# The next-to-last batch's output products: 8 plain single-precision matmuls in place of 24 split ones, with the weight sums made by GpSimd

## Chip, cores and metric

One core of one Trainium2 chip runs the whole kernel in one launch. The metric is the device time in microseconds; every time given for a kernel is a median over runs.

## The reference, cut to what matters

Sixteen sequences (here: batches) of 256 positions and 256 features go through two layers. In each, a normalised input goes through a mixing part `s` and a gate `g`, and `x + s * g` is the result. Layer 0 has a linear recurrence and an MLP. Layer 1, where the change lies, has causal attention over latents with 16 heads, and a gate of a dense product with LoRA experts:

```
kv = (c_kv @ Wkv_b).reshape(B, S, N_HEADS, QK_NOPE + V_DIM)
k_nope, v = (kv[..., :QK_NOPE], kv[..., QK_NOPE:])
...
attn = jax.nn.softmax(scores, axis=-1)
out = jnp.einsum('bhqk,bkhd->bqhd', attn, v).reshape(B, S, N_HEADS * V_DIM)
return out @ Wo
```

The kernel folds `Wkv_b`'s value part into `Wo` once (the folded weight lies in SBUF as 8 rows of 128x256), so that per batch it multiplies attention weights with the 64 latents of each position, and the result (1024 x 256 positions) with the folded weight. That last step is the output product.

## The kernel before

Every engine has one straight program; they meet through named semaphores alone. [...] A product of two single-precision matrices is done in one of two ways. In the split way each operand is a high part in float32r (names `_hi`, `h`) and a low part, the rest (names `_lo`, `l`), and `three` issues three float32r matmuls: low by high, high by low, high by high. In the plain way one float32 matmul does it (scores, transposes, attention by latents); the profile records a plain float32 matmul as two records.

Layer 1 runs in steps `n`, ten per batch (`UNITS`), 160 for the 16 batches, and a tail up to step 173. A step holds one unit of scores (a head pair's block of query rows) and whatever the tables put beside it. Batches overlap: while batch b's units of scores go, the queries of b+1 are made, the keys of b+1, the normalised input of b+2, and the latents and outputs of b-1. The unit kinds are W (2 tiles of 224 and 256 columns), M (3 tiles: 128, 160, 192) and T (transposed). For the batches 14 and 15 the table `LAST` gives the steps by hand: V (attention by latents), L (eviction of the latents), O (output product), R (gating) and C (residual).

Per unit n, in order: TensorE's `l1_s(n)` writes the scores into PSUM; VectorE's `most(n)` adds the mask, takes row minima and writes `SM`; ScalarE's `exps(n)` takes exponentials and their sums; VectorE's `inverse(n)` (two steps later); GpSimd's `normalise(n)` (same step), 2 or 3 instructions; VectorE's `turn_weights(n)` (four steps after the unit), which transposes into `PT`; then, when the units of a batch are all there, TensorE's `l1_pv`. `l1_s(n)` waits until `most(n-2)` is done.

Output, per batch and half of the positions (`qt`): ScalarE's `latents` evicts two banks each for two pairs into `oh` (high part), VectorE's `latents_low` subtracts that from PSUM into `ol` (low part), and `l1_out` makes the product, 8 rows of weight by 3 matmuls of 256 columns. `gated_out`, `residual` and a DMA follow. The products of batch 14 are numbers 28 and 29 (steps 159 and 161), those of batch 15 numbers 30 and 31. On TensorE the tail reads: scores 157, 158, 159; product 28; attention of batch 15, first part; product 29; attention of batch 15, last part; products 30 and 31.

Rotated queries go another way: VectorE's `turn_queries(b, g)` writes `QA`, GpSimd's `queries_sum` adds in place, and SyncE's `place` copies both sums of a half of the heads into `QT` with 8 DMAs, all on one semaphore (`d0` for the first half of batch 15). Here is the wait by which VectorE reuses `QA`:

```
w.wait_ge(*moved(turned[r - 2] // 2))
```

For sum g of batch 15, with g = 2 in step 147, it is the landing of all 8 DMAs with the sums g = 0 and 1 (GpSimd's steps 143 and 144).

Of the kernel before, what the change touches and what calls it, by code (L numbers as in the profile page):

```python
# [8 lines left out]
F32 = mybir.dt.float32  # L9
F32R = mybir.dt.float32r  # L10
I32 = mybir.dt.int32
ALU = mybir.AluOpType
ACT = mybir.ActivationFunctionType
AX = mybir.AxisListType

NB = 16
T = 256
D = 256
# [37 lines left out]
Q0_AT = {}  # L56
LAST_LORA, LAST_SUM, LAST_SPREAD = 152, 153, 149
FIRST_LORA, FIRST_SUM = 5, 6
KV_AT, GATE_AT, SCALE_AT, NORM_AT, YN_AT = 1, 2, 6, 0, 4
TURN_AT, TM_AT, TK_AT, LORA_AT, MISC_AT = 6, 6, 8, 8, (8, 9)  # L60
GATE_REST, FIRST_REST = 9, 22
# [23 lines left out]
    "wrl", "wnl", "wml", "lbl", "mtl", "wol", "bn1", "yn", "ytl", "kv", "kvw", "gt", "gsub", "gf", "z1", "w1",  # L85
    "st", "mx", "r", "qa", "pt", "otl", "ob",

    "gated", "clean", "par", "cs", "nu", "rr", "rt", "fill", "rl", "lr", "kr", "kvr", "n", "qq", "nw", "rs", "oc", "kwk", "kwv",
)


# [113 lines left out]
def build(nc, x, consts, rows, vecs, w1t, w2t, b1c, bt, ct, nuth, wqn, wkbt, wqr, wkva, wvbt, wo,  # L205
          baset, lorab, loraa, routert, out):
    ctx = ExitStack()
    with ctx:
# [112 lines left out]
        w1b = [spare[3], sb("w1b1", [128, 4, 128], F32, l1)]  # L321
        l1.close()

        PS = ctx.enter_context(nc.psum_tensor("bank", [128, 8, 512], F32))
        bank = [PS[:, i, :] for i in range(8)]
        tbank, fbank, obank, ubank, wbank = bank[0], (bank[1], bank[2]), (bank[4], bank[3], bank[6]), bank[5], bank[7]
# [20 lines left out]
        def freed_by(kind, i):  # L347
            if kind == "q":
                return [("qa", g_nth[i // 2]) if i % 2 else ("qn", n_nth[i // 2])]
            if kind == "v":  # L350
                last = max(EVAC.index((qt, i % 4 // 2)) for qt in range(2))
                return [("oth", 4 * (i // 4) + last + 1), ("otl", 4 * (i // 4) + last + 1)]
            if kind == "pad":
                return freed_by(*jorder[i - RING])
            return {"o": [("ob", i + 1)], "ty": [("yth", i + 1), ("ytl", i + 1)], "mi": [("mi", i + 1)],
                    "tk": [("kt", i + 1)], "tm": [("mt", i + 1), ("mtl", i + 1)], "lo": [("z1", i + 1)]}[kind]
# [28 lines left out]
        def evacuated(b, qt):  # L385

            return 4 * b + max(EVAC.index((qt, pair)) for pair in range(2)) + 1

        def normed_rows(b):

# [2 lines left out]
        def by_head(t, pair):  # L393
            return t[:, 4 * pair:4 * pair + 4, :].rearrange("p (i u) t -> p i u t", i=2)
# [158 lines left out]
        def _(e):  # L553
# [232 lines left out]
            def l1_pv(b, blocks, units):  # L786

                first, end = blocks
                C = C4[b % 2]
                w.wait_ge("pt", UNITS * b + units)  # L790
                w.wait_ge(f"c{b % 2}", 256 * (b // 2 + 1))
                for i in range(4):
                    free_shared("v", 4 * b + i)
                if blocks == LAST_BLOCKS:

                    w.wait_ge("otl", 4 * b + 2)
                for kb in range(end):
                    q = max(first, kb)
                    at = slice(64 * (kb % 2), 64 * (kb % 2) + 64)
                    for i in range(4):  # L800
                        rows_ = slice(32 * i, 32 * i + 32)
                        sums = jof("v", 4 * b + i).rearrange("p (u t) -> p u t", u=2)
                        for half in range(2):
                            j = e.matmul(sums[64 * half:64 * half + 64, :, 32 * q:32 * end],  # L804
                                         C[rows_, kb // 2, at], PT[rows_, 2 * half:2 * half + 2, kb, q:end, :],
                                         start=(kb == 0), stop=(kb == end - 1), skip_group_check=True)
                j.then_inc(SEM["pv"], 1)

            def l1_out(k):
                bk, qt = jof("o", k), k % 2  # L810
                w.wait_ge("oth", evacuated(k // 2, qt))
                w.wait_ge("otl", evacuated(k // 2, qt))
                w.wait_ge("woh", 4)
                w.wait_ge("wol", 4)
                free_shared("o", k)
                for c in range(8):
                    i = three(bk[:, 0:256], oh[qt][:, c, :], ol[qt][:, c, :], woe_hi[:, c, :], woe_lo[:, c, :],
                              c == 0, c == 7)
                i.then_inc(SEM["o"], 1)
# [113 lines left out]
        def _(e):  # L933
# [142 lines left out]
            def latents(b, qt):  # L1076
                w.wait_ge("pv", b + 1 + (b == NB - 1 and qt))
                if b == 0:
                    after_l0(w)
                for pair in range(2):  # L1080
                    i = EVAC.index((qt, pair))
                    w.wait_ge("o", 2 * (b - 1) + qt + 1)
                    if i > 1:
                        w.wait_ge("otl", 4 * b + i - 1)
                    e.activation(by_head(oh[qt], pair), latent_pair(b, qt, pair), ACT.Copy).then_inc(SEM["oth"], 1)

            def normed(b):
                w.wait_ge("rs", b + 1 if b > 1 else 1)
# [143 lines left out]
        def _(e):  # L1232
# [579 lines left out]
            for n in range(STEPS):  # L1812
                b, m = n // UNITS, n % UNITS
                for qt in range(2):
                    if (d := due("L", n, qt)) is not None:
                        latents_low(d, qt)
                c, i = divmod(n - 1, UNITS)
                if 0 <= c < NB - 2 and i == TURN_AT:
# [44 lines left out]
        def _(e):  # L1863
# [250 lines left out]
            def residual(k):  # L2114
                w.wait_ge("ob", k + 1)
                e.tensor_tensor(fo[k % 2][:, :], fo[k % 2][:, :], X[:, k, :], ALU.add).then_inc(SEM["oc"], 1)

            chain = iter(())
            for g in range(L0_STEPS):
                if g == 67:  # L2120
# [30 lines left out]
            for n in range(STEPS):  # L2151
# [17 lines left out]
                        residual(2 * d + qt)  # L2169
                if 0 <= n - 2 < TOTAL:  # L2170
                    normalise(n - 2)


def shape_constants():
# [86 lines left out]
```

## Time and profile before

| what | value |
|---|---|
| median of 3 runs | 789.76 us (789.55 to 789.94) |
| the profiled execution's own time | 789.47 us |
| its span (first to last instruction) | 787.7 us |
| busy share: PE, DVE, ACT, POOL | 99%, 86%, 66%, 61% |
| granted TensorE clock, mean | 1.000 (the 2.4 GHz level) |

PE is TensorE's matmuls, PEld its weight loads (beside the matmuls), DVE VectorE, ACT ScalarE, POOL GpSimd, SPq SyncE's queue of DMA issues. Times in rows are microseconds from the span's start unless they are in ns. A matmul record's own duration overlaps with its successor's; the pace is the distance between starts.

### The profile page before, as it was taken

The page shows a single profiled execution, that of the slowest core. Times are in us where ns is not written, and L with a number is a line of the kernel's source. Part 1 is how long each engine was busy: PE and PEld are TensorE (multiplying, and loading weights), DVE is VectorE, ACT ScalarE, POOL GpSimd, SP SyncE. Part 2 cuts the span into 40 slices and gives each one's busy share as a digit, 9 for nine tenths or more (in the row PEclk, how much of TensorE's full clock was granted, in tenths as well). Part 3 has the DMA queues.
Part 4 walks back from the last instruction along what each step waited for, and adds up shares of the span by engine and source line. Part 5 has one row for each costly group of instructions (what it writes and reads, how often), then busy time and mean ns, then how long its engine had stood idle before and what let it go on. Part 6 is the DMA issues. An engine that isn't in the chain of part 4 may idle for free.

```text
span 787.7 us, 23150 instructions
## 1 busy us (share of the span) xinstructions
PE 777.5 (99%) x7976; PEld 710.9 (90%) x7976; DVE 676.5 (86%) x2616; ACT 518.8 (66%) x1610; POOL 480.2 (61%) x1278
## 2 busy tenths in 40 slices
PE   9999999999999999999999999999999999999988
PEld 7889889888899989898998989999898998989867
DVE  6999897888687999888888988989889888989885
ACT  5554454545546687777768777687777768777682
POOL 6880202202236696776867668686776867767673
PEclk9999999999999999999999999999999999999999
DMA  8600220000002223222222322223222222322220
GB/s 305 252 2 1 60 78 34 1 1 1 1 15 50 47 42 58 54 54 36 49 49 45 60 45 52 39 46 58 53 55 35 48 43 49 58 48 53 34 52 28
DMA packets 101335, 41.16 MB, mean 52 GB/s; under 512 B 91745, under 2 KB 98401, under 8 KB 100577
## 3 DMA queue, kind: packets, MB, share of 16 engines
q1 hardware_dynamic: 99984, 39.15, 22.4%
q8 instruction: 63, 1.03, 0.5%
q10 hardware_dynamic: 1232, 0.52, 0.3%
q14 instruction: 56, 0.45, 0.2%
HBM read 14.47 MB, written 4.19 MB: 24 GB/s over the span
## 4 chain that ended last, share of the span: by engine, by line
PE 87%; DVE 5%; SPq 2%; POOL 2%; issue 1%; ACT 1%; DMA 1%; POOLq 0%; DVEq 0%; ACTq 0%
PE bank L558 60%; PE bank L782 11%; PE bank L804 8%; PE bank L775 2%; PE bank L638 2%; SPq L448 1%; SPq L519 1%; PE bank L575 1%; DVE SM L1612 1%; POOL SM L2054 1%; PE bank L690 1%; DVE PT L1635 1%; DVE QA L1583 1%; PE bank L650 1%; DVE ol L1657 1%
## 5 line engine op out<-in xcount | busy, mean ns | idle before, releaser
L1072 ACT ACTIVATE SM<-SM,stb 128x224 f32<-128x224 f32 (+7 forms) x512 | 206.0, 404 | 47.6 <-DVE stb L1612 47.0
L2054 POOL TENSOR_SCALAR SM<-SM,stb 128x224 f32<-128x224 f32 (+7 forms) x512 | 196.3, 406 | 53.8 <-DVE stb L1619 52.4
L558 PE MATMUL bank<-yh,wq_lo 128*128 128x256 f32 x512 | 150.3, 294 | 0.0
L558 PE MATMUL bank<-yh,wq_hi 128*128 128x256 f32 x512 | 144.3, 282 | 0.0
L558 PE MATMUL bank<-yl,wq_hi 128*128 128x256 f32 x512 | 144.2, 282 | 0.0
L782 PE MATMUL bank<-KT,QT 128*128 128x192 f32 (+4 forms) x640 | 118.6, 327 | 2.1 <-DVE stb L1612 2.1
L1635 DVE STREAM_TRANSPOSE PT<-SM 128x128 f32<-128x128 f32 (+2 forms) x232 | 99.3, 459 | 17.4 <-PE bank L804 17.4
L1612 DVE CUSTOM_DVE_ANT_0 SM<-bank,CONST 128x224 f32<-128x224 f32 (+3 forms) x320 | 97.1, 347 | 14.2 <-PE bank L782 10.3
L782 PEld LDWEIGHTS bank<-KT,QT 128*128 128x128 f32 x640 | 98.4, 190 | 6.2 <-DVE stb L1612 3.7
L558 PEld LDWEIGHTS bank<-yh,wq_lo 128*128 128x128 f32 x512 | 96.8, 189 | 1.4
L558 PEld LDWEIGHTS bank<-yl,wq_hi 128*128 128x128 f32 x512 | 96.8, 189 | 0.0
L558 PEld LDWEIGHTS bank<-yh,wq_hi 128*128 128x128 f32 x512 | 96.8, 189 | 0.0
L1072 ACT ACTIVATION_READ_ACCUMULATOR SM<-SM,stb 128x1 f32 x512 | 96.3, 188 | 0.0
L957 ACT ACTIVATE hs<-bank,B 128x512 f32<-128x512 f32 x64 | 43.9, 687 | 78.3 <-PE bank L558 77.3
L1044 ACT ACTIVATE QT<-bank 64x512 f32<-64x512 f32 x128 | 75.4, 589 | 7.2 <-issue 5.4
L1583 DVE TENSOR_TENSOR QA<-bank,TR 128x512 f32<-128x512 f32 x124 | 79.3, 681 | 0.3 <-DMA QT<-QA 0.3
L2047 POOL TENSOR_TENSOR QA<-QA 128x256 f32<-128x256 f32 x62 | 46.4, 749 | 53.9 <-DVE QA L1583 53.9
L558 PE MATMUL bank<-woe_hi,ol 128*128 128x256 f32 x256 | 75.4, 294 | 0.7 <-issue 0.7
L558 PE MATMUL bank<-w2h,hl 128*128 128x256 f32 x256 | 74.2, 290 | 0.3 <-DVE w2l L1356 0.2
L558 PE MATMUL bank<-w2h,hh 128*128 128x256 f32 x256 | 72.4, 283 | 0.0
L558 PE MATMUL bank<-w2l,hh 128*128 128x256 f32 x256 | 72.3, 283 | 0.0
L558 PE MATMUL bank<-woe_hi,oh 128*128 128x256 f32 x256 | 72.1, 282 | 0.0
(227 smaller groups left out, 2056.4 us busy)
## 6 DMA issues: line engine op xcount, KB each, us to landing
QT<-QA SPq DMA_DIRECT2D x244, 64.0 KB, 2.1
PT<-KV SPq DMA_DIRECT2D x256, 16.0 KB, 1.8
out<-fo SPq DMA_DIRECT2D x32, 128.0 KB, 2.0
X<-in_x SPq DMA_DIRECT2D x7, 512.0 KB, 11.0
stage<-in_wqn SPq DMA_DIRECT2D x2, 1024.0 KB, 5.2
stage<-in_wo SPq DMA_DIRECT2D x2, 1024.0 KB, 5.0
stage<-in_w1t SPq DMA_DIRECT2D x4, 256.0 KB, 5.3
stage<-in_w2t SPq DMA_DIRECT2D x2, 512.0 KB, 7.0
```

The costliest lines, as they stand in the source:

```text
L558: i = e.matmul(dst, a, b, start=(first and j == 0), stop=(last and j == 2), skip_group_check=skip)
L638: i = e.matmul(ubank[:, 256 * j:256 * j + 256], Z[b][:, 128 * j:128 * j + 128], RR[:, :], start=True, stop=True)
L782: j = e.matmul(sbank[n % 2][:, at], Q[:, q, :, :].rearrange("p h c -> p (h c)"), KT[b % 3][:, p, 0:32 * q + 32], start=True, stop=True)
L804: j = e.matmul(sums[64 * half:64 * half + 64, :, 32 * q:32 * end], C[rows_, kb // 2, at], PT[rows_, 2 * half:2 * half + 2, kb, q:end, :], ...
L957: e.activation(hs[g % 2][:, :], fbank[g % 2][:, :], ACT.Gelu, bias=B1[:, g % 8:g % 8 + 1]).then_inc(SEM["gelu"], 1)
L1044: i = e.activation(QT[r, (2 * b + g // 2) % 3, p, :, g % 2:4:2, :].rearrange("p n j c -> p j n c"), src[r, :, :, :], ACT.Copy)
L1072: i = e.activation(M[:, at], M[:, at], ACT.Exp, bias=S[:, 0, j:j + 1], scale=-1.0, accum_out=S[:, 1, j:j + 1])
L1583: i = e.tensor_tensor(A[:, part, :, :, g % 2, :], src, TR[:, part, :].rearrange("p (n c) -> p n c", n=8).unsqueeze(1).broadcast_to([128, 2 ...
L1612: i = e.tensor_tensor_reduce(M[:, at], bk[:, at], mask[:, 224 - 32 * q:256], 1.0, 3e38, ALU.add, ALU.min, S[:, 0, j:j + 1])
L1635: return e.transpose(PT[:, slot, 0:k, q:q + some, :].rearrange("p k q c -> p q k c"), src)
L2047: e.tensor_tensor(A[:, 0, 0, :, :], A[:, 0, 0, :, :], A[:, 1, 1, :, :], ALU.subtract)
L2054: i = e.tensor_scalar(P[:, at], P[:, at], S[:, 2, j:j + 1], 1.0, ALU.mult, ALU.mult)
```

## The change

For batch 14 alone, ScalarE evicts the latents in full single precision into `of` (which lies where `ol` did), VectorE's four subtractions go, and products 28 and 29 are 8 plain float32 matmuls each, of `of` with `whole`. `whole` is the folded weight in full, `woe_hi + woe_lo`, made by GpSimd in eight additions of 128x256, one at the end of each of its steps 141 to 148, in SBUF in which `yh1`, `yl1`, `yn0` and `yn1` have been used up by then. The counts on semaphore `otl` shift for batch 15 accordingly.

```diff
@@ -56,6 +56,7 @@
 Q0_AT = {}
 LAST_LORA, LAST_SUM, LAST_SPREAD = 152, 153, 149
 FIRST_LORA, FIRST_SUM = 5, 6
+WHOLE_AT = 141
 KV_AT, GATE_AT, SCALE_AT, NORM_AT, YN_AT = 1, 2, 6, 0, 4
 TURN_AT, TM_AT, TK_AT, LORA_AT, MISC_AT = 6, 6, 8, 8, (8, 9)
 GATE_REST, FIRST_REST = 9, 22
@@ -321,6 +322,17 @@
         w1b = [spare[3], sb("w1b1", [128, 4, 128], F32, l1)]
         l1.close()
 
+
+
+        l2 = ExitStack()
+        sb("gap3", [128, 512], F32, l2)
+        whole = [sb("whole0", [128, 2, D], F32, l2)]
+        sb("gap4", [128, 512], F32, l2)
+        whole += [sb(f"whole{i}", [128, 2, D], F32, l2) for i in range(1, 4)]
+        sb("gap5", [128, 28384], F32, l2)
+        of = [sb(f"of{i}", [128, 8, 128], F32, l2) for i in range(2)]
+        l2.close()
+
         PS = ctx.enter_context(nc.psum_tensor("bank", [128, 8, 512], F32))
         bank = [PS[:, i, :] for i in range(8)]
         tbank, fbank, obank, ubank, wbank = bank[0], (bank[1], bank[2]), (bank[4], bank[3], bank[6]), bank[5], bank[7]
@@ -349,7 +361,9 @@
                 return [("qa", g_nth[i // 2]) if i % 2 else ("qn", n_nth[i // 2])]
             if kind == "v":
                 last = max(EVAC.index((qt, i % 4 // 2)) for qt in range(2))
-                return [("oth", 4 * (i // 4) + last + 1), ("otl", 4 * (i // 4) + last + 1)]
+                if i // 4 == NB - 2:
+                    return [("oth", 4 * (i // 4) + last + 1)]
+                return [("oth", 4 * (i // 4) + last + 1), ("otl", lows(i // 4, last + 1))]
             if kind == "pad":
                 return freed_by(*jorder[i - RING])
             return {"o": [("ob", i + 1)], "ty": [("yth", i + 1), ("ytl", i + 1)], "mi": [("mi", i + 1)],
@@ -385,6 +399,11 @@
         def evacuated(b, qt):
 
             return 4 * b + max(EVAC.index((qt, pair)) for pair in range(2)) + 1
+
+        def lows(b, k):
+
+
+            return 4 * (b - (b == NB - 1)) + k
 
         def normed_rows(b):
 
@@ -793,7 +812,7 @@
                     free_shared("v", 4 * b + i)
                 if blocks == LAST_BLOCKS:
 
-                    w.wait_ge("otl", 4 * b + 2)
+                    w.wait_ge("otl", lows(b, 2))
                 for kb in range(end):
                     q = max(first, kb)
                     at = slice(64 * (kb % 2), 64 * (kb % 2) + 64)
@@ -809,7 +828,15 @@
             def l1_out(k):
                 bk, qt = jof("o", k), k % 2
                 w.wait_ge("oth", evacuated(k // 2, qt))
-                w.wait_ge("otl", evacuated(k // 2, qt))
+                if k // 2 == NB - 2:
+                    w.wait_ge("whole", 8)
+                    free_shared("o", k)
+                    for c in range(8):
+                        i = e.matmul(bk[:, 0:256], of[qt][:, c, :], whole[c // 2][:, c % 2, :], start=(c == 0),
+                                     stop=(c == 7))
+                    i.then_inc(SEM["o"], 1)
+                    return
+                w.wait_ge("otl", lows(k // 2, evacuated(k // 2, qt) - 4 * (k // 2)))
                 w.wait_ge("woh", 4)
                 w.wait_ge("wol", 4)
                 free_shared("o", k)
@@ -1080,9 +1107,10 @@
                 for pair in range(2):
                     i = EVAC.index((qt, pair))
                     w.wait_ge("o", 2 * (b - 1) + qt + 1)
-                    if i > 1:
-                        w.wait_ge("otl", 4 * b + i - 1)
-                    e.activation(by_head(oh[qt], pair), latent_pair(b, qt, pair), ACT.Copy).then_inc(SEM["oth"], 1)
+                    if i > 1 and b != NB - 2:
+                        w.wait_ge("otl", lows(b, i - 1))
+                    to = of[qt] if b == NB - 2 else oh[qt]
+                    e.activation(by_head(to, pair), latent_pair(b, qt, pair), ACT.Copy).then_inc(SEM["oth"], 1)
 
             def normed(b):
                 w.wait_ge("rs", b + 1 if b > 1 else 1)
@@ -1812,7 +1840,7 @@
             for n in range(STEPS):
                 b, m = n // UNITS, n % UNITS
                 for qt in range(2):
-                    if (d := due("L", n, qt)) is not None:
+                    if (d := due("L", n, qt)) is not None and d != NB - 2:
                         latents_low(d, qt)
                 c, i = divmod(n - 1, UNITS)
                 if 0 <= c < NB - 2 and i == TURN_AT:
@@ -2114,6 +2142,13 @@
             def residual(k):
                 w.wait_ge("ob", k + 1)
                 e.tensor_tensor(fo[k % 2][:, :], fo[k % 2][:, :], X[:, k, :], ALU.add).then_inc(SEM["oc"], 1)
+
+            def whole_row(c):
+                w.wait_ge("lo", NB - 1)
+                w.wait_ge("ty", NB)
+                w.wait_ge("q", max(q_nth[8 * (NB - 2) + u] for u in range(8)))
+                e.tensor_tensor(whole[c // 2][:, c % 2, :], woe_hi[:, c, :].bitcast(F32), woe_lo[:, c, :].bitcast(F32),
+                                ALU.add).then_inc(SEM["whole"], 1)
 
             chain = iter(())
             for g in range(L0_STEPS):
@@ -2169,6 +2204,8 @@
                         residual(2 * d + qt)
                 if 0 <= n - 2 < TOTAL:
                     normalise(n - 2)
+                if WHOLE_AT <= n < WHOLE_AT + 8:
+                    whole_row(n - WHOLE_AT)
 
 
 def shape_constants():
```

GpSimd's program in steps 142 to 144, before (`QA` is `queries_sum`, `SM` is `normalise`, of units 141 and, further on, 142):

```order
L2047 TENSOR_TENSOR QA<-QA 128x8x32 [waits qa]
L2048 TENSOR_TENSOR QA<-QA 128x8x32
L2054 TENSOR_SCALAR SM1<-SM1,stb1 128x128 [waits r]
L2054 TENSOR_SCALAR SM1<-SM1,stb1 128x160
L2054 TENSOR_SCALAR SM1<-SM1,stb1 128x192
L2047 TENSOR_TENSOR QA<-QA 128x8x32 [waits qa]
L2048 TENSOR_TENSOR QA<-QA 128x8x32
```

and now:

```order
L2150 TENSOR_TENSOR whole0<-woe_hi,woe_lo 128x256
L2075 TENSOR_TENSOR QA<-QA 128x8x32 [waits qa]
L2076 TENSOR_TENSOR QA<-QA 128x8x32
L2082 TENSOR_SCALAR SM1<-SM1,stb1 128x128 [waits r]
L2082 TENSOR_SCALAR SM1<-SM1,stb1 128x160
L2082 TENSOR_SCALAR SM1<-SM1,stb1 128x192
L2150 TENSOR_TENSOR whole1<-woe_hi,woe_lo 128x256
L2075 TENSOR_TENSOR QA<-QA 128x8x32 [waits qa]
L2076 TENSOR_TENSOR QA<-QA 128x8x32
```

The second and third of the additions stand ahead of the two sums of queries; the first stands 8 instructions further up.

GpSimd's program in steps 147 to 149, before (`SM1` is unit 146, `SM2` unit 147, `fo` a residual):

```order
L2054 TENSOR_SCALAR SM1<-SM1,stb2 128x32 [waits r]
L2054 TENSOR_SCALAR SM1<-SM1,stb2 128x64
L2054 TENSOR_SCALAR SM1<-SM1,stb2 128x96
L2054 TENSOR_SCALAR SM1<-SM1,stb2 128x32
L2054 TENSOR_SCALAR SM1<-SM1,stb2 128x64
L2054 TENSOR_SCALAR SM1<-SM1,stb2 128x96
L2116 TENSOR_TENSOR fo0<-fo0,X 128x256 [waits ob]
L2054 TENSOR_SCALAR SM2<-SM2,stb3 128x128 [waits r]
L2054 TENSOR_SCALAR SM2<-SM2,stb3 128x160
L2054 TENSOR_SCALAR SM2<-SM2,stb3 128x192
```

and now:

```order
L2150 TENSOR_TENSOR whole3<-woe_hi,woe_lo 128x256
L2082 TENSOR_SCALAR SM1<-SM1,stb2 128x32 [waits r]
L2082 TENSOR_SCALAR SM1<-SM1,stb2 128x64
L2082 TENSOR_SCALAR SM1<-SM1,stb2 128x96
L2082 TENSOR_SCALAR SM1<-SM1,stb2 128x32
L2082 TENSOR_SCALAR SM1<-SM1,stb2 128x64
L2082 TENSOR_SCALAR SM1<-SM1,stb2 128x96
L2150 TENSOR_TENSOR whole3<-woe_hi,woe_lo 128x256
L2144 TENSOR_TENSOR fo0<-fo0,X 128x256 [waits ob]
L2082 TENSOR_SCALAR SM2<-SM2,stb3 128x128 [waits r]
L2082 TENSOR_SCALAR SM2<-SM2,stb3 128x160
L2082 TENSOR_SCALAR SM2<-SM2,stb3 128x192
```

The last two additions stand ahead of the normalisation of unit 146 and of unit 147; nothing else moved.

TensorE's program at product 28 (step 159), before, its first four of 24 matmuls behind the last scores:

```order
L782 MATMUL bank<-KT0,QT 128x256
L558 MATMUL bank<-woe_hi,ol0 128x256 [waits z1,otl,oth]
L558 MATMUL bank<-woe_lo,oh0 128x256
L558 MATMUL bank<-woe_hi,oh0 128x256
L558 MATMUL bank<-woe_hi,ol0 128x256
```

and now, 5 of its 8:

```order
L801 MATMUL bank<-KT0,QT 128x256
L835 MATMUL bank<-whole0,of0 128x256 [waits z1,whole,oth]
L835 MATMUL bank<-whole0,of0 128x256
L835 MATMUL bank<-whole1,of0 128x256 x2
L835 MATMUL bank<-whole2,of0 128x256 x2
```

The wait on `otl` (VectorE's subtractions) is gone, that on `whole` has come, and each row of weight takes one matmul in place of three.

## Rows read from the trace of the kernel before

**Rows 1.** The page: busy time and share of the span, by engine.
```profile
PE 777.5 (99%) x7976; PEld 710.9 (90%) x7976; DVE 676.5 (86%) x2616; ACT 518.8 (66%) x1610; POOL 480.2 (61%) x1278
```

**Rows 2.** Busy time in stretches of the end: length, then engines, clock, DMA.
```profile
750.00:760.00 10.00, 9.61 (x191) 7.58 (x193) 8.94 (x53) 8.66 (x38) 7.76 (x18) 1.00 0.27 46
760.00:770.00 10.00, 7.98 (x82) 6.33 (x65) 9.50 (x52) 9.00 (x37) 5.55 (x17) 1.00 0.14 38
```

**Rows 3.** The chain that ended last: start, us, what.
```profile
742.05 1.21 DVE QA L1583 x2
...
743.34 0.74 POOL QA L2047
...
746.16 3.50 POOL SM L2054 x12
...
769.95 0.76 DVE PT L1635 x2
...
770.75 2.60 PE bank L804 x92
773.36 3.04 PE bank L558 x24
```

**Rows 4.** GpSimd's additions of 128x256, all of a line: ns min/median/max.
```profile
L2047 POOL TENSOR_TENSOR QA<-QA x62: 721/736/1159, 239.7 to 744.7; 128x256 f32<-128x256 f32 x62
...
L2116 POOL TENSOR_TENSOR fo<-fo,X x32: 723/738/779, 309.6 to 784.7; 128x256 f32<-128x256 f32 x32
```

**Rows 5.** GpSimd's timeline: start, us; in brackets idle time before it.
```profile
729.03 0.73 POOL L2047 TENSOR_TENSOR QA<-QA 128x256 f32<-128x256 f32 x1
...
732.21 0.74 POOL L2048 TENSOR_TENSOR QA<-QA 128x256 f32<-128x256 f32 x1
...
734.02 0.64 POOL L2041 TENSOR_TENSOR ML<-ML,lg 128x256 f32<-128x256 f32 x1
737.23 0.91 POOL L2054 TENSOR_SCALAR SM<-SM,stb 128x224 f32<-128x224 f32 x2 [2.56 <-DVE stb L1619]
739.57 1.16 POOL L2054 TENSOR_SCALAR SM<-SM,stb 128x128 f32<-128x128 f32 x3 [1.43 <-DVE stb L1619]
...
750.31 1.17 POOL L2054 TENSOR_SCALAR SM<-SM,stb 128x128 f32<-128x128 f32 x3
```

**Rows 6.** The 8 DMAs of `place`, 732 to 745: ns, first and last start, us to landing.
```profile
L448 SPq DMA_DIRECT2D QT<-QA x8: 591/611/1915, 733.0 to 738.8; - x8
...
DMA to landing us min/median/max: 2.1/2.1/3.6
```

**Rows 7.** VectorE's timeline.
```profile
750.50 0.17 DVE L1619 RECIPROCAL stb<-stb 128x2 f32<-128x2 f32 x1 [0.94 <-ACT SM L1072]
...
751.97 0.75 DVE L1635 STREAM_TRANSPOSE PT<-SM 128x128 f32<-128x128 f32 x2
...
753.92 0.18 DVE L1619 RECIPROCAL stb<-stb 128x3 f32<-128x3 f32 x1 [0.49 <-ACT SM L1072]
...
766.17 1.29 DVE L1657 TENSOR_TENSOR ol<-bank,oh 128x512 fp32r<-128x512 f32 x2 [0.45 <-ACT oh L1085]
...
768.68 1.28 DVE L1657 TENSOR_TENSOR ol<-bank,oh 128x512 fp32r<-128x512 f32 x2
```

**Rows 8.** The chain, where TensorE alone makes it: plain scores, then split queries.
```profile
719.76 1.63 PE bank L782 x10
721.39 2.84 PE bank L558 x24
```

**Rows 9.** TensorE's timeline.
```profile
738.01 0.38 PE L715 MATMUL bank<-CONST,ML 128*128 128x128 f32 x2
...
765.77 1.08 PE L782 MATMUL bank<-KT,QT 128*128 128x224 f32 x4 [0.23 <-DVE stb L1612]
767.56 0.36 PE L558 MATMUL bank<-woe_hi,ol 128*128 128x256 f32 x1 [0.71 <-issue]
```

**Rows 10.** ScalarE's timeline: its eviction of batch 14's first half.
```profile
765.54 1.08 ACT L1085 ACTIVATE oh<-bank 128x512 fp32r<-128x512 f32 x2
```

More of the change, by code:

```diff
@@ L86 @@
     "st", "mx", "r", "qa", "pt", "otl", "ob",
-    "gated", "clean", "par", "cs", "nu", "rr", "rt", "fill", "rl", "lr", "kr", "kvr", "n", "qq", "nw", "rs", "oc", "kwk", "kwv",
+    "whole", "gated", "clean", "par", "cs", "nu", "rr", "rt", "fill", "rl", "lr", "kr", "kvr", "n", "qq", "nw", "rs", "oc", "kwk", "kwv",
 )
```

## The prediction

> **What bounds the kernel now.** First the page: TensorE is busy in 99% of the span, VectorE in 86% [rows 1], so a step counts where TensorE is on the path or waits. Then the stretches of the end: TensorE has work in 9.61 of 10 us from 750 to 760 and in 7.98 of 10 from 760 to 770, while VectorE has 9.50 there [rows 2]. The change lies around this stretch. Then the chain that ended last: from 742 it is not on TensorE. It runs through VectorE's turn of the queries (742.05), GpSimd's sums of queries (743.34) and GpSimd's normalisations (from 746.16), back to VectorE, and reaches TensorE only at 770.75, with the attention of batch 15; product 29 is on it with 3.04 us [rows 3]. So TensorE sets the pace until about 750, the pair of VectorE and GpSimd from 742 to 770, TensorE after that. Last the timelines, for the slack at each place that the change touches.
>
> **GpSimd's eight additions.** The trace has 94 additions of this size in SBUF, at a median of 0.74 us each [rows 4]. Behind one another they start 0.70 apart: four of them fill 743.34 to 746.16 [rows 3]. I price each at 0.70.
> - The first three (2.1 us) stand ahead of the second sum of queries of batch 15. GpSimd has no idle time from 729.03 to 734.66 [rows 5], so that sum, which ends at 732.95, ends at 735.05. SyncE starts its 8 DMAs at once (733.0); the last starts at 738.8 and lands 2.1 us later, at 740.9 [rows 6]. VectorE's next turn of queries waits for all of them and began at 742.05 [rows 3]: a cover of 1.1 us against 2.1. VectorE is late by 1.0, and GpSimd's sums of 743.34 with it.
> - The fourth makes the gate product, which ended at 734.66 [rows 5], end 2.8 later, at 737.5. TensorE transposes it at 738.01 [rows 9]: hidden, with 0.5 to spare.
> - The fifth and sixth fall beside idle time: 2.56 us before 737.23, of which the fourth leaves nothing to wait for, 1.43 before 739.57, and 2.6 from 740.73 to 743.34 [rows 3, 5]. Hidden.
> - The seventh and eighth stand ahead of the normalisations of units 146 and 147, in a stretch in which GpSimd is on the chain [rows 3]: 1.4 us. With the 1.0 from above, unit 147's normalisation, which ends at 751.48 [rows 5], ends 2.4 late. VectorE took it up at 751.97 [rows 7]: 0.5 is slack, so VectorE is 1.9 late there. Its next wait, 0.49 before 753.92, is for ScalarE [rows 7], whose exponentials of unit 150 need minima that come 0.8 late and still end before VectorE is back; it swallows 0.49. Left over: 1.4. The 0.94 of idle time before 750.50 [rows 7] helps unit 146 alone (1.7 late at GpSimd, 0.8 at VectorE), since it comes ahead of unit 147. Behind it VectorE has work without a gap to 765.7, and ScalarE's exponentials follow VectorE's minima, so 1.4 is the lateness of everything up to 766.
>
> **Product 28.** TensorE started it at 767.56, when two subtractions of VectorE (from 766.17) were done [rows 7, 9]. Without that wait it needs ScalarE's eviction, ended by 766.6 [rows 10], and the last scores, which take 0.81 from 765.77 [rows 8, 9], 766.6 as well. That is 0.96 earlier by itself; with 1.4 of lateness it starts at 768.0.
> Its length: 10 records of plain scores, 5 matmuls with 960 columns in all, took 1.63 us, which is 1.70 ns a column, and 24 split matmuls of 256 columns 2.84 [rows 8]. Eight plain ones have 2048 columns, 3.48 us. The old product took 3.04 from start to start [rows 3], 0.20 over the bare 2.84; with the same 0.20 the new one takes 3.68: 0.64 more. The bounds: no dearer than now (3.04), or, if the loading of weights between plain matmuls showed, as far above 3.68 as that is above 3.04 (4.3). I take 3.68, since scores are the same instruction at nearly the same shape.
> The attention of batch 15 then starts at 768.0 + 3.68 = 771.7. Before, it was 770.75, where VectorE's turn of the weights (769.95, 0.76 long) released it [rows 3], 0.15 after TensorE was free (767.56 + 3.04). That turn comes at about 769.6 now, since the four subtractions, 0.6 us each [rows 7], are gone ahead of it: covered. The shift there is 1.4 - 0.96 + 0.64 - 0.15 = +0.93. So the subtractions' 2.4 us of VectorE buy 0.96 + 0.15, because the product waits for ScalarE next.
>
> **Product 29 and the end.** TensorE goes from attention to product 29 to attention without a wait [rows 3]; 0.64 more. Products 30 and 31 and what surrounds them stay. ScalarE writes `of` in place of `oh`, at the same size: 0, and a difference of 0.1 would be seen once. Together +0.93 + 0.64 = +1.57 us: the profiled execution's 789.47 would become 791.0, and since that one lies 0.29 below the median of 789.76, the median becomes 791.3.
>
> **A rule that speaks against the change.** The slowest of the 62 additions of L2047 took 1.159 us [rows 4], the medians 0.74. The Trainium skill, GPSIMD Engine Reference, section 1, says that GpSimd shares its SBUF interfaces with VectorE and contends with VectorE instructions that read two SBUF inputs; in section 4.1, that an elementwise addition is about twice as slow there as on VectorE. By the rows the eight additions stay near 0.74; by that rule some could near 1.16, which is the second rival.
>
> **The rivals.** Within 0.2% (1.6 us) is about what a measurement of this kernel can't tell from no change.
> - *The first link is covered.* If the sums of queries or the DMAs absorb the first three additions, only the 1.4 of the last two come in: 1.4 - 0.5 - 0.49 = 0.44 late, and the sum is 0.44 - 0.96 + 0.64 - 0.15 + 0.64 = +0.6, 790.4. For it: the cover is 1.1 of 2.1. Against: one semaphore counts all eight DMAs. 20%.
> - *The additions are dearer.* At 1.16 each (1.12 from start to start) the DMAs land 3.4 late, VectorE is 2.3 late at 742, GpSimd 4.5 at unit 147, VectorE 3.5 behind it: 3.5 - 0.96 + 0.64 - 0.15 + 0.64 = +3.7, 793.4; the gate product, 4.5 late, would then hold TensorE at 738 for 1.1, in parallel. Half of the way is 792.4. For it: 1.159 in the row. Against: the medians. 15%.
> - *Faster: the shorter tail shows.* The mechanism is the lost wait for the subtractions, at product 28. If GpSimd's lateness is hidden throughout and a plain product takes no longer than a split one, the attention starts at 766.6 + 3.04 = 769.6, 1.1 earlier, and so does the end: 788.7. With lateness 0 the sign turns where a product takes 3.6 (-1.1 + 2 x 0.55 = 0), and my 3.68 is just beyond. For it: VectorE's 9.50 of 10 us there. Against: rows 3, 5 and 8, as read above. 8%, of which most is below 0.2%.
> - *Nothing shows.* Lateness 0 and products at 3.68: +0.2, 789.9. 7%.
> - *The forecast*, +1.57 give or take 0.5: 50%.
>
> **How the numbers follow.** The forecast alone has 790.8 to 791.8; its middle lies right at the bound of 0.2% (791.34), so I split its 50% into 27 within and 23 slower. Slower: 23 + 15 = 38%. Faster by over 0.2%: 5%, out of the third rival (with products at 2.8 or less). Same: 27 + 20 + 7 + 3 = 57%. The range goes from 789.7, which takes in the first rival and the fourth, to 792.5, which takes in half of the second: about 83%.
>
> **What would show it.** In the profile of the changed kernel: eight GpSimd additions at 0.74; VectorE's turn of batch 15's third sum idle for about 1 us on a DMA near 742; VectorE idle on GpSimd before the turn of unit 147's weights; TensorE's idle time ahead of the first tail product ended by ScalarE, not VectorE; 16 records of float32 per product over 3.5 us; the first attention of batch 15 released by TensorE itself. It is wrong if the DMAs of that half land before VectorE asks for them, if GpSimd's steps 147 to 149 had slack that I didn't see, or if a plain product costs other than 3.68.

## The result, and the profile after

The changed kernel takes 791.35 us (median of 22 runs) beside 790.02 for the one before (22 runs of the same sitting): a ratio of 1.0017, interval 1.0011 to 1.0023, or +1.33 us. The forecast was +1.57 and 791.3. The number came out, in part by luck: two steps of the working failed, one too dear by 1.0 and one too cheap by 0.64, and most of that cancelled. That even the 791.3 was hit has a second piece of luck in it, since the kernel before came 0.26 higher in this sitting than the 789.76 that the forecast started from.

One run of the changed kernel took 1978 us, and one of the kernel before, beside the experiments, 953; the comparisons leave both out, and their cause isn't known.

The spans of the two profiled executions, 787.7 and 789.6, differ by 1.9 us, which is more than the change makes. The chain shows where the rest is from:

```profile
720.37 1.63 PE bank L801 x10
...
743.30 1.22 DVE QA L1611 x2
744.59 0.73 POOL QA L2075
...
749.84 1.74 POOL SM L2082 x6
751.58 0.70 POOL whole L2150
...
752.98 1.13 POOL SM L2082 x3
...
768.58 3.54 PE bank L835 x16
...
778.31 1.92 PE bank L823 x119
```

The first line is the same ten records of scores that stood at 719.76 in [rows 8], before anything that the change touches can have reached TensorE: this execution is 0.61 us late there already. Each profile of this study has such an offset (-0.2 to +1.1 us where nothing upstream was changed), so every shift below is a difference to before of the start of the thing named, less the difference of these ten records. By it the last part of the attention, which follows product 29, starts 1.30 us late.

The two windows of [rows 2], after:

```profile
750.00:760.00 10.00, 8.80 (x132) 6.88 (x138) 7.99 (x50) 7.68 (x29) 8.79 (x22) 1.00 0.34 57
760.00:770.00 10.00, 8.68 (x125) 6.64 (x110) 9.34 (x56) 9.34 (x42) 7.40 (x21) 1.00 0.15 40
```

The columns are as in [rows 2]. From 750 to 760 GpSimd (last busy column) rose from 7.76 to 8.79 us and TensorE fell from 9.61 to 8.80, VectorE from 8.94 to 7.99. In this window VectorE now waits 1.3 us for GpSimd's normalisations, where it waited for none of them before, and TensorE 1.1 us for VectorE's minima, where it was 0.4. The granted clock is 1.00 in both windows of both kernels, the 2.4 GHz level. So no clock is in the difference.

The new products and what is around them, in TensorE's timeline, and the eviction ahead of them in ScalarE's:

```profile
767.50 1.08 PE L801 MATMUL bank<-KT,QT 128*128 128x224 f32 x4 [0.23 <-DVE stb L1640]
768.41 3.71 PE L835 MATMUL bank<-whole,of 128*128 128x256 f32 x16
772.05 2.61 PE L823 MATMUL bank<-PT 32*64 32x384 f32 x96
774.59 3.72 PE L835 MATMUL bank<-whole,of 128*128 128x256 f32 x16
778.24 1.99 PE L823 MATMUL bank<-PT 32*64 32x128 f32 x128
```

```profile
767.26 1.08 ACT L1113 ACTIVATE of<-bank 128x512 f32<-128x512 f32 x2
```

Product 28 takes 3.64 us from start to start, product 29 3.65. The idle time of 0.71 that stood ahead of product 28 in [rows 9] is gone: it starts 0.91 behind the last scores' start.

Then the first hop of the chain, at 743.30. SyncE's DMAs of [rows 6], VectorE around its turn of the queries, and GpSimd:

```profile
L467 SPq DMA_DIRECT2D QT<-QA x8: 591/610/611, 735.7 to 740.2; - x8
...
DMA to landing us min/median/max: 2.1/2.1/2.1
```

```profile
739.03 0.64 DVE L1640 CUSTOM_DVE_ANT_0 SM<-SM,CONST 128x32 f32<-128x32 f32 x1
...
739.93 0.18 DVE L1640 CUSTOM_DVE_ANT_0 SM<-SM,CONST 128x32 f32<-128x32 f32 x1
...
742.15 0.38 DVE L1640 CUSTOM_DVE_ANT_0 SM<-SM,CONST 128x32 f32<-128x32 f32 x1
...
743.22 2.48 DVE L1611 TENSOR_TENSOR QA<-bank,TR 128x512 f32<-128x512 f32 x4
```

```profile
738.89 0.73 POOL L2150 TENSOR_TENSOR whole<-woe_hi,woe_lo 128x256 f32<-128x256 f32 x1
740.63 1.15 POOL L2082 TENSOR_SCALAR SM<-SM,stb 128x128 f32<-128x128 f32 x3 [1.01 <-DVE stb L1647]
741.75 0.74 POOL L2150 TENSOR_TENSOR whole<-woe_hi,woe_lo 128x256 f32<-128x256 f32 x1
```

Read them together. The last DMA starts at 740.2 and lands 2.1 us later, 742.3, and VectorE does not reach its turn of the queries until 743.22: nothing waited for the DMAs. But the instruction by which VectorE takes the minima of a transposed unit's first tile, `SM<-SM,CONST` of 128x32, took 0.64 us at 739.03 and 0.38 at 742.15, where its twin at 739.93 took 0.18. Before, both took the short time (the third row, at a later place, is taken up at the end):

```profile
738.42 0.19 DVE L1612 CUSTOM_DVE_ANT_0 SM<-SM,CONST 128x32 f32<-128x32 f32 x1
...
741.09 0.19 DVE L1612 CUSTOM_DVE_ANT_0 SM<-SM,CONST 128x32 f32<-128x32 f32 x1
...
759.61 0.40 DVE L1612 CUSTOM_DVE_ANT_0 SM<-SM,CONST 128x32 f32<-128x32 f32 x1
```

0.64 and 0.38 against 0.19 twice is 0.64 more, and VectorE's turn of the queries shifts by 0.64. The long ones lie beside the fifth and the sixth of GpSimd's additions (738.89 and 741.75) and end 0.05 and 0.04 us behind the ends of those (739.67 to 739.62, 742.53 to 742.49). I call that a hold. It lies where the prediction had written "hidden".

Further on VectorE stands for unit 147's normalisation, which the seventh and eighth addition put off, as forecast:

```profile
754.13 0.77 DVE L1663 STREAM_TRANSPOSE PT<-SM 128x128 f32<-128x128 f32 x2 [1.03 <-POOL SM L2082]
```

### The profile page after: what moved, and what is told of

It reads as the page before. It is cut to its first block, busy times and chain, and to the rows that moved or that the text cites. A ratio compares the mean times of both kernels' runs of the same rounds, so it can differ in the third digit from the quotient of the medians.

```text
span 789.6 us, 23121 instructions
## 1 busy us (share of the span) xinstructions
PE 778.8 (99%) x7960; PEld 711.0 (90%) x7960; DVE 679.3 (86%) x2612; ACT 518.4 (66%) x1610; POOL 484.7 (61%) x1286
## 4 chain that ended last, share of the span: by engine, by line
PE 89%; DVE 5%; POOL 2%; issue 1%; DMA 1%; ACT 1%; SPq 1%; ACTq 0%; POOLq 0%; DVEq 0%
PE bank L577 61%; PE bank L801 12%; PE bank L823 8%; PE bank L794 2%; PE bank L657 2%; DVE SM L1640 1%; PE bank L594 1%; PE bank L835 1%; PE bank L709 1%; DVE QA L1611 1%; POOL SM L2082 1%; DVE PT L1663 1%; PE bank L669 1%; SPq L467 1%; PE bank L683 1%
## 5 line engine op out<-in xcount | busy, mean ns | idle before, releaser
L577 PE MATMUL bank<-woe_hi,ol 128*128 128x256 f32 x240 | 70.7, 295 | 0.0
L823 PE MATMUL bank<-PT 32*64 32x128 f32 (+7 forms) x2144 | 67.8, 396 | 0.0
```

What stands on the lines that cost most here:

```text
L577: i = e.matmul(dst, a, b, start=(first and j == 0), stop=(last and j == 2), skip_group_check=skip)
```

## The experiments

Theory A, after these rows: the cost is two holds (0.64) and two additions on the chain (1.4, less 0.49 and 0.46 swallowed behind), then 0.6 for each plain product, less what the missing subtractions give back. Theory B, the rival: the recorded way of the prediction, by the landing of DMAs, or nothing from the additions at all. For each run the table has the shifts against before, as explained above: VectorE's turn of batch 15's third sum of queries; ScalarE's first eviction of batch 14's latents; the start of product 28; the start of the last part of the attention ("end"); then the ratio of times to the kernel before with its interval.

| run | turn of queries | eviction | product 28 | end | ratio |
|---|---|---|---|---|---|
| changed kernel | +0.64 | +1.11 | +0.25 | +1.30 | 1.0017 [1.0011, 1.0023] |
| the same, again | +0.65 | +1.07 | +0.20 | +1.26 | 1.0018 [1.0010, 1.0027] |
| additions only | +0.71 | +1.21 | +1.21 | +1.20 | 1.0013 [1.0004, 1.0022] |
| products only | 0 | 0 | -0.88 | +0.18 | 0.9998 [0.9989, 1.0007] |
| last two late | +0.70 | +0.71 | -0.16 | +0.90 | 1.0015 [1.0006, 1.0024] |
| one input | +0.77 | +1.52 | +0.65 | +1.71 | 1.0018 [1.0009, 1.0027] |
| early | 0 | -0.03 | -0.90 | +0.16 | 1.0025 [1.0017, 1.0034] |
| early, 28 alone | 0 | -0.03 | -0.90 | +0.15 | 1.0025 [1.0015, 1.0035] |
| halves | +1.49 | +2.22 | +1.35 | +2.41 | 1.0037 [1.0024, 1.0051] |
| no hold | +0.10 | +0.60 | -0.27 | +0.78 | 1.0011 [1.0002, 1.0020] |
| fitted, both | 0 | 0 | -0.87 | +0.19 | 0.9999 [0.9990, 1.0007] |
| fitted, 28 alone | 0 | -0.01 | -0.88 | -0.43 | 0.9996 [0.9987, 1.0005] |

An interval of the ratio is about 0.7 us to either side in most rows, so the trace, aligned, tells these runs apart where the times can't. The two early runs lose another 1.43 us ahead of the instruction by which they are aligned, which the shifts leave out. With that added, every time agrees with its trace inside its interval. The shifts are good to 0.01, and each rests on one profiled execution; that the changed kernel gave +1.30 and +1.26 in two tells how far they repeat.

**Additions only, products only.** The change in two halves. In the first, products 28 and 29 and the subtractions are as before and the sums are made and not used:

```diff
-                if k // 2 == NB - 2:
-                    w.wait_ge("whole", 8)
-                    ...
```

> The kernel before with GpSimd's eight additions at their places and nothing else: both products of batch 14 stay split, with VectorE's subtractions. Theory A (GpSimd's lateness is the main cost): VectorE is held by the fifth and sixth addition for 0.65 us at the minima of units 145 and 146, the seventh and eighth bring 1.4, slack takes 0.5 and 0.45, so the end is 1.1 us later than before. Theory B (the additions are hidden, the dearer plain products are the cost): 0, within 0.2 of before.

In the second the additions are left out, and the plain products take `woe_hi` in place of `whole`, so the low part of the weight is missing:

```diff
-                    w.wait_ge("whole", 8)
+                    w.wait_ge("woh", 4)
...
-                if WHOLE_AT <= n < WHOLE_AT + 8:
-                    whole_row(n - WHOLE_AT)
```

> The changed kernel without GpSimd's additions: the plain products read the high part of the weight in place of the whole one, so the low part is left out. Theory A: the wait saved is worth 0.96 + 0.15, two products cost 0.64 more each, so +0.2 us against before; product 28 starts some 1.0 earlier than before and takes 3.65 from start to start. Theory B: the products are the cost, +1.3. A third: if the shorter tail were worth more than the products cost, below 0.

Additions alone: +1.20 at the end, as A has it, with the same two holds, in VectorE's timeline:

```profile
738.74 0.70 DVE L1630 CUSTOM_DVE_ANT_0 SM<-SM,CONST 128x32 f32<-128x32 f32 x1
...
741.91 0.38 DVE L1630 CUSTOM_DVE_ANT_0 SM<-SM,CONST 128x32 f32<-128x32 f32 x1
```

Products alone: +0.18, and no hold. TensorE's timeline:

```profile
766.47 3.71 PE L835 MATMUL bank<-woe_hi,of 128*128 128x256 f32 x16
770.11 2.61 PE L823 MATMUL bank<-PT 32*64 32x384 f32 x96
```

Product 28 starts 0.88 earlier than before and takes 3.64. The halves add up to 1.38, beside 1.30 for the whole. B's "nothing from the additions" falls.

The changed kernel itself went once more, beside later runs:

> The changed kernel as it is, beside the other three on the same chip: +1.3 us against before. Theory A as to its parts: SyncE's eight issues follow one another at 0.65 us without the pause that the kernel before has at the third, the first minima of units 145 and 146 are held, and product 28 takes 3.65 from start to start.

It gave the same two holds and +1.26.

**Last two late.** The seventh and eighth additions go from steps 147 and 148 to 153 and 154, off the chain; the first six stay.

```diff
-WHOLE_AT = 141
+WHOLE_STEPS = (141, 142, 143, 144, 145, 146, 153, 154)
```

> The changed kernel with the seventh and eighth addition at steps 153 and 154, where GpSimd was idle for 1.7 us each, in place of 147 and 148. Theory A: only the hold of 0.65 is left ahead of unit 147, and the slack of 0.5 and 0.45 there swallows it, so the end is +0.2 to +0.4 us against before (VectorE can be held once more, by up to 0.7, at the minima of units 153 and 154). Theory B: no difference to the changed kernel, +1.3.

It came out at +0.90, above what was expected, though unit 147's lateness fell from 2.01 to 0.68. VectorE's and GpSimd's timelines at the new place of the eighth:

```profile
760.87 0.80 DVE L1640 CUSTOM_DVE_ANT_0 SM<-SM,CONST 128x64 f32<-128x64 f32 x1
761.61 0.08 DVE L1640 DVE_READ_ACCUMULATOR2_ANT stb<- 128x1 f32 x1
```

```profile
760.87 0.73 POOL L2150 TENSOR_TENSOR whole<-woe_hi,woe_lo 128x256 f32<-128x256 f32 x1
```

There the addition, put into idle time of GpSimd again, met the minima of another transposed unit: 0.80 in place of 0.22, and the lateness, 0.1 by then, was back at 0.7. So the miss is itself a hold, at a place where no chain through GpSimd ran.

**No hold.** The fifth and sixth additions wait until VectorE has taken the minima of units 145 and 146. Nothing else differs from the changed kernel.

```diff
+                    if n in (145, 146):
+                        w.wait_ge("mx", n + 1)
```

> The changed kernel, but the fifth and sixth addition wait until the minima of units 145 and 146 are written. Theory A: both first minima instructions are back at 0.19 us, VectorE's turn of queries starts 0.65 earlier, only the 1.4 of the seventh and eighth addition are left, less 0.5 and 0.45 of slack, and the end is +0.6 us against before in place of +1.3. Rival (the stretched minima are chance): +1.3.

VectorE's timeline:

```profile
738.63 0.19 DVE L1640 CUSTOM_DVE_ANT_0 SM<-SM,CONST 128x32 f32<-128x32 f32 x1
...
741.30 0.28 DVE L1640 CUSTOM_DVE_ANT_0 SM<-SM,CONST 128x32 f32<-128x32 f32 x1
```

The turn of the queries is 0.10 late in place of 0.64, and the end +0.78 in place of +1.30: the two holds cost 0.5 us of the change's 1.3. This is the direct test: the same eight additions, moved by one wait, and the first link is gone. (0.28 is what is left, beside a normalisation of GpSimd; it is half of what the end lies above the expected 0.6. The other half wasn't traced.)

**One input.** To see whether it is the addition's two inputs in SBUF that hold VectorE, a copy of the high part takes its place (the low part is left out):

```diff
-                e.tensor_tensor(whole[c // 2][:, c % 2, :], woe_hi[:, c, :].bitcast(F32), woe_lo[:, c, :].bitcast(F32),
-                                ALU.add).then_inc(SEM["whole"], 1)
+                e.tensor_scalar(whole[c // 2][:, c % 2, :], woe_hi[:, c, :].bitcast(F32), 1.0, None,
+                                ALU.mult).then_inc(SEM["whole"], 1)
```

> The changed kernel with each addition replaced by a GpSimd copy of the high part (one tensor input, the same size; the low part of the weight is left out). If VectorE is held because both engines read two SBUF inputs: the first minima instruction of units 145 and 146 is back at 0.19 us (0.64 and 0.38 in the changed kernel), the copies take about 0.5, GpSimd is 0.9 to 1.0 late at unit 147, slack takes it, and the end is +0.2 to +0.4 us. If any GpSimd instruction holds VectorE: the minima instruction still ends where the copy ends, and the end is +0.5 or more.

The copies, by line, two of them in GpSimd's timeline, and VectorE's timeline:

```profile
L2150 POOL TENSOR_SCALAR whole<-woe_hi x8: 849/860/873, 728.2 to 752.3; 128x256 f32<-128x256 f32 x8
```

```profile
739.98 0.86 POOL L2150 TENSOR_SCALAR whole<-woe_hi 128x256 f32<-128x256 f32 x1
...
742.51 0.85 POOL L2150 TENSOR_SCALAR whole<-woe_hi 128x256 f32<-128x256 f32 x1
```

```profile
739.48 0.95 DVE L1640 CUSTOM_DVE_ANT_0 SM<-SM,CONST 128x32 f32<-128x32 f32 x1
...
740.36 0.21 DVE L1640 CUSTOM_DVE_ANT_0 SM<-SM,CONST 128x64 f32<-128x64 f32 x1
...
740.51 0.25 DVE L1640 CUSTOM_DVE_ANT_0 SM<-SM,CONST 128x96 f32<-128x96 f32 x1
...
742.91 0.19 DVE L1640 CUSTOM_DVE_ANT_0 SM<-SM,CONST 128x32 f32<-128x32 f32 x1
```

The copy takes 860 ns where the addition takes 735, so that everything on GpSimd moved, and the end is +1.71. Four instructions of the minima lie wholly beside a copy, the three at 740.36, 740.51 and 742.91 above and one of 0.22 at 743.03, and all have their short times (0.21 or 0.22 for 128x64, 0.25 for 128x96, 0.19 for 128x32). So the copy, which has one input in SBUF, did not hold them, where an addition held such an instruction to its end. One row stays unread: the very first minima took 0.95, beside two normalisations that end at 740.03 and then 0.45 us of a copy. As for the time, the experiment missed its aim: the copies are too long for the end to say anything.

**Halves.** Each addition as two of 128x128. If a hold lasts until GpSimd's current instruction ends, shorter instructions make it shorter.

```diff
+                for half in (slice(0, 128), slice(128, 256)):
+                    i = e.tensor_tensor(whole[c // 2][:, c % 2, half], woe_hi[:, c, half].bitcast(F32),
+                                        woe_lo[:, c, half].bitcast(F32), ALU.add)
+                i.then_inc(SEM["whole"], 1)
```

> The changed kernel with each addition in two halves of 128x128. If a held VectorE instruction waits for the end of the GpSimd instruction then running: the first minima instruction of unit 145 takes at most 0.45 us in place of 0.64 to 0.70, and that of unit 146 at most 0.4. If it waits until GpSimd has a pause: 0.9 and 0.6, since two halves take longer than one whole. By theory A the end follows GpSimd's time: the halves take some 0.2 more per addition at the seventh and eighth, +1.3 to +1.8 us against before.

It went the other way. VectorE's timeline, then GpSimd's:

```profile
739.02 1.35 DVE L1640 CUSTOM_DVE_ANT_0 SM<-SM,CONST 128x32 f32<-128x32 f32 x1
...
742.84 0.52 DVE L1640 CUSTOM_DVE_ANT_0 SM<-SM,CONST 128x32 f32<-128x32 f32 x1
```

```profile
738.58 0.90 POOL L2082 TENSOR_SCALAR SM<-SM,stb 128x224 f32<-128x224 f32 x2
739.45 0.87 POOL L2151 TENSOR_TENSOR whole<-woe_hi,woe_lo 128x128 f32<-128x128 f32 x2
741.33 1.14 POOL L2082 TENSOR_SCALAR SM<-SM,stb 128x128 f32<-128x128 f32 x3 [1.01 <-DVE stb L1647]
742.43 0.88 POOL L2151 TENSOR_TENSOR whole<-woe_hi,woe_lo 128x128 f32<-128x128 f32 x2
```

The first minima began beside the normalisations, went through their end (739.48), through both halves (to 740.32), and ended 0.05 us behind the second. So a hold isn't always over with the instruction that began it: this one went on over two more that followed without a gap. (In the run with the last two late one did end where a normalisation gave way to an addition: 760.54, 0.40 us. What decides between the two isn't shown.) The end is +2.41: the holds cost 1.49 at the turn of the queries, and the two halves of an addition take 0.87 where a whole one takes 0.73.

**Early.** All eight additions ahead of the stretch, in steps 130 to 139, with the products as in the change; and the same with product 28 alone plain, whose latents' second half keeps its split form.

```diff
-WHOLE_AT = 141
+WHOLE_STEPS = (130, 131, 132, 133, 134, 137, 138, 139)
```

> The changed kernel with the eight additions at GpSimd's steps 130 to 134 and 137 to 139 (their buffers are free by then), while TensorE alone makes the chain. Theory A: their lateness and their holds of VectorE end in slack there, nothing is late at 766, and the end is +0.2 us against before, 1.1 ahead of the changed kernel. Rival: the stretch up to 727 has no slack either, TensorE waits there for minima, and the end is +1 us or more.

> As e5, and product 28 alone is plain; product 29 is split as before, with VectorE's two subtractions. Theory A: product 28 starts 0.96 earlier and costs 0.64 more, the attention behind it is 0.5 earlier, product 29 costs what it did: -0.45 us against before. Rival (VectorE's two subtractions that are left hold the attention or product 29): 0 to +0.3.

Both took 2 us more than before, for a reason ahead of the stretch. The waits of the first from 640 to 750:

```profile
PE bank L734 <- POOL ML L2069: 1.3, 1, 1.3
```

TensorE, which is the bound there, stood 1.3 us (from 704.4) for the gate product of the batch before, put off by the additions ahead of it. Against before, the first is 1.11 us late ahead of this place and 2.54 behind it, the second 0.47 and 1.90: 1.43 us each. That is the wait that the prediction's step on the fourth addition had left 0.5 us short of happening; here more additions stood ahead of it. Behind that, the first ends at +0.16, like the products alone. The second should have ended 0.45 earlier and ended at +0.15: ScalarE's second eviction now had to wait for a subtraction of VectorE's (by a wait that I wrote too strictly), the second subtraction for that eviction, and VectorE's turn of the weights stood behind it. TensorE's timeline and VectorE's:

```profile
768.57 3.71 PE L833 MATMUL bank<-whole,of 128*128 128x256 f32 x16
772.80 2.61 PE L821 MATMUL bank<-PT 32*64 32x384 f32 x96 [0.53 <-DVE PT L1661]
```

```profile
771.32 0.69 DVE L1683 TENSOR_TENSOR ol<-bank,oh 128x512 fp32r<-128x512 f32 x1 [0.66 <-ACT oh L1111]
```

The attention starts 4.23 us behind product 28 in place of 3.64, which is the 0.6 missing. The price of one plain product was not reached by this run; the fitted one below does that.

**Fitted.** The additions where neither holds nor the gate product are touched: two behind the minima of step 136, two in step 140, three in 145, one behind the minima of 146. Once with both products plain, once with product 28 alone.

```diff
-WHOLE_AT = 141
+WHOLE_AHEAD, WHOLE_BEHIND = {140: (2, 3), 145: (4, 5, 6)}, {136: (0, 1), 146: (7,)}
```

> The same placing of the additions, and both products plain. Theory A: what the products alone cost is left, +0.2 us against before, as in the run with the products only.

> Additions fitted into GpSimd's idle time and away from the transposed units' minima: two at step 136 behind unit 136's minima, two at step 140 and three at step 145 ahead of the normalisation, one at step 146 behind unit 146's minima. Product 28 alone is plain; product 29 is split, and ScalarE's second eviction of that half doesn't wait for VectorE. Theory A: no hold, nothing late at 766, product 28 0.96 earlier and 0.64 dearer, the attention 0.5 earlier, product 29 as before: -0.45 us against before. Rival: what is left of VectorE's subtractions or the additions still delays: 0 to +0.5.

Both as expected in the trace. TensorE's timeline of the second (its offset is +0.73):

```profile
767.41 3.71 PE L833 MATMUL bank<-whole,of 128*128 128x256 f32 x16
771.05 2.60 PE L821 MATMUL bank<-PT 32*64 32x384 f32 x96
773.59 0.39 PE L575 MATMUL bank<-woe_hi,ol 128*128 128x256 f32 x1
```

With product 28 alone plain the end lies 0.43 us ahead of before: -0.88 for the earlier start, +0.60 for the length, -0.15 for the wait behind it. The time, 789.65 beside 789.88, ratio 0.9996 [0.9987, 1.0005], cannot tell that from nothing. It is the only version here whose trace beats the kernel before.

## Why the prediction held, and which steps of it did not

- **"VectorE is late by 1.0", by the landing of the DMAs: wrong.** The premise was right: the sums came 2.1 late (SyncE's first DMA starts 735.66, less 0.61, against 732.98: +2.07). But the step took over SyncE's timing as it was before, the slowest of 1915 ns in [rows 6] included. That slow issue is absent after, the longest is 611 ns, and the last DMA lands 0.9 us ahead of VectorE. In all runs with the sums over 2 us late (changed kernel twice, additions only, last two late, one input, halves, no hold) none of the eight issues is slow; in those with the sums in time (before, products only, early, both fitted) one takes 0.97 to 1.92 us. So it goes with the time at which the sums come, and the trace shows what lies there: a transfer of 0.02 MB that the profile calls `instruction`, on queue q8. Here it is before (it starts between 734.2 and 734.3, at the long issue of 734.27) and after (734.84 to 735.77):

```profile
q8 instruction: 1, 0.02, 6.1%
...
q8 instruction: 1, 0.02, 5.8%
```

Less the offset it comes at the same time in both, 734.23, and with the sums 2.1 late it is all but over when SyncE's first DMA starts. In each of the six runs with a long issue, that issue overlaps such a transfer. No run moved the transfer by itself, so that it makes the issue long is not tested. The forecast's 1.0 was measured as 0. With all eight issues at the 0.65 from start to start that the others have, the prediction's own times give it: 735.05 + 7 x 0.65 + 2.1 = 741.7, ahead of 742.05. By the prediction's own sign (the DMAs land before VectorE asks for them) this link failed, and that the number held in spite of it is luck.
- **"The fifth and sixth ... Hidden": wrong.** They fit GpSimd's idle time, as forecast, and cost 0.64 by holding VectorE, the engine that had none. The step looked for who waits for GpSimd and not for who runs beside it. Shown by the run without the hold (+0.10 in place of +0.64) and by the additions alone.
- **The rule quoted against the change**, the Trainium skill, GPSIMD Engine Reference, section 1, on contention with VectorE instructions that read two SBUF inputs, was weighed on the wrong side. I asked whether GpSimd's additions would get longer; they did not (718 to 742 ns, beside the median of 736 in [rows 4]). VectorE's instruction did, and it is one with both inputs in SBUF. The trace agrees with the rule, with 0.64 in place of 0.19.
- **The fourth, and the gate product: right.** TensorE transposes the gate product at 738.61, as before with the offset, without a wait. The early runs show that the cover behind this step was real and small.
- **The seventh and eighth: right.** 0.64 + 1.39 = 2.03; measured 2.01 late at the end of unit 147's normalisation. Behind it 0.46 of slack was swallowed (forecast 0.5) and 0.49 by the wait for ScalarE (0.49), which leaves 1.06; the eviction is 1.11 late. With 2.4 in place of 2.0 the forecast had 1.4.
- **Product 28 and the gains: right, sizes off by up to 0.1.** Its start gained 0.87 (forecast 0.96), its length is 3.64 (3.68) against 3.04, and the 0.15 wait went. Product 29: +0.61 (0.64). The released wait is ScalarE's, as forecast.
- **The sum:** 1.11 - 0.87 + 0.60 - 0.15 + 0.61 = 1.30, forecast 1.4 - 0.96 + 0.64 - 0.15 + 0.64 = 1.57. The same sum gives the end of each other run with two plain products out of its eviction's shift, to 0.02.
- **The rivals.** "The first link is covered" (+0.6, 20%) was right about its mechanism, and would have been the outcome but for the holds: the run without holds is nearest to it, at +0.78, whose eviction is 0.60 late, not 0.44. The additions weren't dearer (the rows of the kernel before hold more of them than the 94 that the prediction counted, since L2048 makes them too), and the faster case fails on two products at 3.64, just beyond the 3.6 that it named.

## What to carry to other kernels

Work that is put into an engine's idle time is free only if the engines beside it don't mind: look at what else runs in those windows, above all VectorE's instructions with both inputs in SBUF beside a GpSimd stretch, and put the work behind them. A plain single-precision product of 256 columns costs a fifth more of TensorE than the split one (3.64 against 3.04 us), so it pays only where the preparation of the split form ends last, once and not twice. When a term rests on one slow member of a group of rows (here 1915 beside 611 ns), price it both ways, and look what else, `instruction` transfers among it, runs at that moment. And align two traces on an untouched instruction ahead of the change before a difference under a microsecond is read.

## What the runs showed of the hardware

- GpSimd's normalisations and additions, each with two inputs in SBUF, can hold a VectorE instruction that has both inputs in SBUF. Of a 128x32 minima of 0.19 us: 0.64, 0.70 (one addition of 0.73 beside it), 1.35 (a normalisation and two halves). The hold is not a slower pace: in each of these rows VectorE's instruction ends 0.04 to 0.05 us behind the end of a GpSimd instruction, and the 0.80 of the run with the last two late 0.07 behind. The row of 0.95 beside a copy is the one that doesn't fit. It is nothing new of the change: before it, at 759.61, the same instruction takes 0.40 and ends 0.04 behind a normalisation of GpSimd, and in every trace of this study one near 265 takes 0.39 or 0.40 and ends 0.04 to 0.05 behind an addition of the gate (`ML<-ML,lg`).

- GpSimd's copy of 128x256 with one input in SBUF did not hold them: four that lie wholly beside one took 0.19 to 0.25, their usual times.

- VectorE's instructions whose first input is in PSUM (`SM<-bank,CONST`, 0.25 us for 128x128) keep that time beside GpSimd's additions (at 746.31 and 752.24 after the change).
- On GpSimd, a one-input multiplication by a constant of 128x256 took 860 ns and an addition with two inputs 735: fewer inputs weren't faster.
- One of SyncE's eight issues of DMAs takes 0.97 to 1.92 us in place of 0.61 in some kernels and none in others, by the time of the first. In the thirteen traces 183 of the 3172 issues of this kind take over 0.9 us, and 182 of these overlap an `instruction` transfer of q8; of the other 2989 only 268 do. So an overlap goes with a long issue but doesn't always make one.
